# Sharing the group statistics of a normalisation between VectorE and ScalarE: 8 of 32 groups in five of eight chunks

## What is computed

```python
def _gn(v, G=32, eps=1e-5):
    g = v.reshape(B_, H_, W_, G, C_ // G)
    m = jnp.mean(g, axis=(1, 2, 4), keepdims=True)
    s = jnp.var(g, axis=(1, 2, 4), keepdims=True)
    return ((g - m) / jnp.sqrt(s + eps)).reshape(v.shape)

# layer 0: _L0_conv_ref is a layer norm over channels, five projections with sigmoid gates and masks,
#   einsum('bkjd,bkid->bijd', left, right), a layer norm, a projection and an output gate
x = x + _L0_conv_ref(_gn(x), ...)
# layer 1: 12 x 12 Fourier modes, mixed over channels
x = x + _L1_conv_ref(_gn(x), ...)
```

## Time and profile before

| | |
|---|---|
| median of 3 runs | 2864.22 us (2863.98 to 2865.37) |
| the profiled execution | 2871.38 us, its span 2869.6 us |
| granted TensorE clock, mean of the span | 0.959 of full speed |
| VectorE's statistics, first to last instruction | 14.71 to 193.97 us |
| last instruction of `prepare` | 202.12 us + 0.20 |
| DMA bytes moved per second while chunks are loaded | about 410 GB/s |

### The profile page before, as it was taken

How to read it: one execution, slowest core, us unless ns; L and a number is a source line. 1 busy time by engine, 2 the same in 40 slices (tenths; PEclk the granted TensorE clock), 3 DMA queues, 4 the chain that set the end, 5 groups by cost and what they waited for, 6 DMA issues and landing times. The chain is left out here.

```text
span 2869.6 us, 43971 instructions
## 1 busy us (share of the span) xinstructions
PE 2453.6 (86%) x14742; PEld 1996.0 (70%) x14742; DVE 2211.2 (77%) x3468; ACT 1380.6 (48%) x1812; POOL 1022.4 (36%) x1043
## 2 busy tenths in 40 slices
PE   0008999889989979999999998699999989979983
PEld 0007988778878868888888887366665656778872
DVE  6998999779779838888888888777676767427852
ACT  0107999779779966766667676122122222100000
POOL 0019888787788830000000000244444444300000
PEclk9999999999999989999999999799999999859997
DMA  9945999898888877777777777999999999539999
GB/s 384 389 170 189 352 348 351 304 336 303 310 328 310 318 294 264 282 288 274 285 273 283 287 275 277 349 391 416 391 415 392 416 383 393 143 127 388 420 421 411
DMA packets 244984, 927.61 MB, mean 323 GB/s; under 512 B 18009, under 2 KB 21593, under 8 KB 244442
## 3 DMA queue, kind: packets, MB, share of 16 engines
q1 hardware_dynamic: 205912, 796.12, 73.6%
q10 hardware_dynamic: 38898, 129.21, 11.3%
HBM read 527.85 MB, written 394.92 MB: 322 GB/s over the span
## 5 line engine op out<-in xcount | busy, mean ns | idle before, releaser
L1236 POOL TENSOR_TENSOR fi_square_sum<-fi_square_sum,fi_square 128x1024 f32<-128x1024 f32 x128 | 302.9, 2366 | 362.4 <-ACT fi_square L1202 362.4
L717 DVE SCALAR_TENSOR_TENSOR pj_lr<-pj_v_ps,keep_b_val,pj_sig 128x1024 f32<-128x1024 f32 x256 | 328.6, 1284 | 129.0 <-PE pj_v_ps L570 98.4
L1202 ACT ACTIVATE fi_square<-fi_x 128x1024 f32<-128x1024 f32 x128 | 135.4, 1058 | 519.8 <-DVE fi_x L1264 517.3
L510 POOL TENSOR_TENSOR front_ring<-front_ring,front_gn_shift 128x512 f32<-128x512 f32 x256 | 329.9, 1290 | 33.2 <-DVE front_ring L683 33.2
L653 ACT ACTIVATE pj_sig<-pj_g_ps,keep_b_gate 128x1024 f32<-128x1024 f32 x256 | 285.9, 1117 | 43.1 <-PE pj_g_ps L570 38.2
L1157 PE MATMUL fi_y_ps<-fi_scaled,keep_w_bd 128*128 128x512 f32 x512 | 273.4, 616 | 31.6 <-DVE fi_scaled L1247 31.1
L909 PE MATMUL ct_acc_ps<-ct_l_hi,ct_r_hi 128*128 128x512 f32 x1024 | 281.0, 395 | 17.4 <-ACT ct_r_hi L932 17.4
L913 PE MATMUL ct_acc_ps<-ct_l_lo,ct_r_hi 128*128 128x512 f32 x1024 | 280.8, 395 | 0.0
L917 PE MATMUL ct_acc_ps<-ct_l_hi,ct_r_lo 128*128 128x512 f32 x1024 | 280.1, 394 | 0.0
L1247 DVE TENSOR_TENSOR fi_scaled<-fi_m,fi_s_ps 128x512 f32<-128x512 f32 x256 | 174.2, 681 | 136.5 <-DMA fi_m<-mixed_d 127.6
L530 POOL TENSOR_TENSOR front_ring<-front_ring,pj_guess 128x512 f32<-128x512 f32 x256 | 267.4, 1046 | 3.3 <-POOL pj_guess L524 1.6
(11 more groups left out here) (183 smaller groups left out, 6313.2 us busy)
## 6 DMA issues: line engine op xcount, KB each, us to landing
lr_d<-pj_lr SPq DMA_DIRECT2D x128, 1024.0 KB, 6.4
gate_d<-pj_gout SPq DMA_DIRECT2D x128, 512.0 KB, 7.1
ct_l<-lr_d SPq DMA_DIRECT2D x64, 1024.0 KB, 7.0
ct_r<-lr_d SPq DMA_DIRECT2D x64, 1024.0 KB, 9.0
mixed_d<-ct_o SPq DMA_DIRECT2D x64, 1024.0 KB, 5.0
fi_g<-gate_d SPq DMA_DIRECT2D x128, 512.0 KB, 14.9
fi_x<-in_x SPq DMA_DIRECT2D x32, 2048.0 KB, 17.2
fi_m<-mixed_d SPq DMA_DIRECT2D x128, 512.0 KB, 17.6
```

Of the source, the lines that this page charges most:

```text
L510: pool.tensor_tensor(tile(m), tile(m), keep.gn_shift[:, :].unsqueeze(1).to_broadcast([P, WS // 2, C]), ALU.add).then_inc(shifted, 1)
L717: dve.scalar_tensor_tensor(out=out[:, :, RG * (m % 2):RG * (m % 2) + RG], in0=v_ps[:, :].rearrange("p (q i) -> p q i", i=RG), scalar=keep. ...
L1236: pool.tensor_tensor(square_sum[:, :, :], square_sum[:, :, :], square[:, :, :], ALU.add).then_inc(sum_done, 1)
```

## The change

VectorE leaves the last 8 of the 32 groups (`SG` = 8, `WG` = 24) of chunks 2 to 6 (`SHARED`) to ScalarE. For each such chunk and group, ScalarE runs two activations over the same 512 elements: Identity and Square, both with the bias `minus_pivot` (one value per partition and group) and with an accumulated sum (`accum_out`); the element-wise results go to two PSUM banks, `spill`, and are not read. Each activation waits for the one two before it. The pivot is the mean that `bn_stats` found for the first half of chunk 0; two VectorE instructions write it after chunk 0. ScalarE takes chunk 2 before its wait for `products`, and chunks 3 to 6 after its weight copies. The load of chunk i + 2 now also waits for ScalarE's part of chunk i (`spilled`).

Before the second half of chunk 7, VectorE turns the sums into means and sums of squared deviations and writes them into the slots of `stats` that `bn_stats` would have filled (`merge_shared`, 10 instructions). Chunk 6 is now taken in halves too, so `stats` has 12 slots: 8 of halves, 4 of wholes.

```diff
-HALVED = (0, 1, NCHUNK - 1)
+HALVED = (0, 1, NCHUNK - 2, NCHUNK - 1)
+SHARED = list(range(2, NCHUNK - 1))
+SG = 8
+WG = G - SG
...
+        spill = [t.ps(f"spill{b}", [P, STATS_T * CG]) for b in range(2)]
...
                 if i >= 2:
                     sp.wait_ge(chunk_done, i - 1)
+                    if i - 2 in SHARED:
+                        sp.wait_ge(spilled, 2 * SG * (SHARED.index(i - 2) + 1))
...
+            def shared(i):
+                b = i % 2
+                k = SHARED.index(i)
+                for h in range(2):
+                    act.wait_ge(x_loaded[b][h], DMA * (i // 2) + DMA)
+                for q in range(SG):
+                    part = xc[b][:, :, CG * (WG + q):CG * (WG + q) + CG]
+                    across = [bank[:, :].rearrange("p (t c) -> p t c", c=CG) for bank in spill]
+                    done = 2 * (SG * k + q)
+                    if done:
+                        act.wait_ge(spilled, done - 1)
+                    act.activation(across[0], part, ACT.Identity, bias=minus_pivot[:, q:q + 1],
+                                   accum_out=act_sum[:, q, k:k + 1]).then_inc(spilled, 1)
+                    if done:
+                        act.wait_ge(spilled, done)
+                    act.activation(across[1], part, ACT.Square, bias=minus_pivot[:, q:q + 1],
+                                   accum_out=act_square[:, q, k:k + 1]).then_inc(spilled, 1)
...
+            act.wait_ge(pivot_ready, 1)
+            shared(SHARED[0])
             act.wait_ge(products, 1)
...
+            for i in SHARED[1:]:
+                shared(i)
             act.wait_ge(root_in, 1)
...
+            def merge_shared():
+                n = CG * STATS_T
+                dve.wait_ge(spilled, 2 * SG * len(SHARED))
+                link(dve.tensor_scalar(act_mean[:, :, :], act_sum[:, :, :], 1.0 / n, None, ALU.mult))
+                link(dve.tensor_tensor(act_sum[:, :, :], act_sum[:, :, :], act_mean[:, :, :], ALU.mult))
+                link(dve.tensor_tensor(act_inner[:, :, :], act_square[:, :, :], act_sum[:, :, :], ALU.subtract))
+                link(dve.tensor_tensor(act_mean[:, :, :], act_mean[:, :, :],
+                                       pivot[:, :].unsqueeze(2).to_broadcast([P, SG, len(SHARED)]), ALU.add))
...
+                for e in (0, 3):
+                    at = slice(first + 1 + e, first + 6 * wholes, 6)
+                    dve.tensor_copy(stats[:, WG:G, at], act_mean[:, :, 0:wholes])
+                    at = slice(first + 2 + e, first + 6 * wholes, 6)
+                    dve.tensor_scalar(stats[:, WG:G, at], act_inner[:, :, 0:wholes], 0.5, None, ALU.mult)
+                for field, table, share in ((1, act_mean, 1.0), (2, act_inner, 0.25)):
...
+                    last = dve.tensor_scalar(stats[:, WG:G, at], whole, share, None, ALU.mult)
+                link(last)
...
             def statistics(i):
+                groups = WG if i in SHARED else G
                 if i in HALVED:
                     for h in range(2):
+                        if i == NCHUNK - 1 and h == 1:
+                            merge_shared()
...
-                        for g in range(G):
+                        for g in range(groups):
...
-            for i in range(3):
+            statistics(0)
+            dve.wait_ge(chunk_done, 1)
+            link(dve.tensor_copy(pivot[:, :], stats[:, WG:G, 1]))
+            dve.tensor_scalar(minus_pivot[:, :], pivot[:, :], -1.0, None, ALU.mult).then_inc(pivot_ready, 1)
+            for i in range(1, 3):
                 statistics(i)
```

More of the change, by code:

```diff
@@ L142, in prepare @@
         inner_sum = t.sb("inner_sum", [P, G])
+        pivot = t.sb("pivot", [P, SG])
+        minus_pivot = t.sb("minus_pivot", [P, SG])
+        act_sum = t.sb("act_sum", [P, SG, len(SHARED)])
+        act_square = t.sb("act_square", [P, SG, len(SHARED)])
+        act_mean = t.sb("act_mean", [P, SG, len(SHARED)])
+        act_inner = t.sb("act_inner", [P, SG, len(SHARED)])
         total = t.sb("total", [P, G])
@@ L150, in prepare @@
         chunk_done = t.sem("chunk_done")
+        pivot_ready = t.sem("pivot_ready")
+        spilled = t.sem("spilled")
         mean_ready = t.sem("mean_ready")
@@ L313, in _ @@
             link = chained(dve, step)
+            def merge_shared():
[6 more added lines that the diff above has]
+                                       pivot[:, :].unsqueeze(2).to_broadcast([P, SG, len(SHARED)]), ALU.add))
+                first = 6 * SPLIT
+                wholes = len(SHARED) - 1
+                halves = 6 * 2 * HALVED.index(SHARED[-1])
+                for e in (0, 3):
[4 more added lines that the diff above has]
+                for field, table, share in ((1, act_mean, 1.0), (2, act_inner, 0.25)):
+                    at = slice(halves + field, halves + 12, 3)
+                    whole = table[:, :, wholes:wholes + 1].to_broadcast([P, SG, 4])
+                    last = dve.tensor_scalar(stats[:, WG:G, at], whole, share, None, ALU.mult)
+                link(last)
             def statistics(i):
                 b, done = i % 2, DMA * (i // 2) + DMA
+                groups = WG if i in SHARED else G
                 if i in HALVED:
                     for h in range(2):
+                        if i == NCHUNK - 1 and h == 1:
+                            merge_shared()
                         dve.wait_ge(x_loaded[b][h], done)
```

## The result

| | before | changed |
|---|---|---|
| median | 2864.80 us (10 runs) | 2857.22 us (10 runs, 2855.45 to 2859.23) |
| ratio | | 0.9974, 95% interval 0.9965 to 0.9984 |
| the profiled execution | 2871.38 us | 2859.01 us |
| first normalisation of `project` in it | 202.89 us | 193.50 us |

The change is faster by 7.6 us, which is 0.26%; by the interval it is between 4.6 and 10.0 us. The prediction was 10.2, and its range (2851.0 to 2858.0) holds the median.

What follows compares the result with a forecast made beforehand. Loads were taken to bound `prepare` until chunk 6, then VectorE. Statistics ending 10.5 us earlier, less 0.4 in the tail, gave 10.2 us off 2864.22: 2854.0 us, range 2851.0 to 2858.0 (80 in 100).

Steps and rivals of the forecast that it cites:

- a part taken back by the merge or behind `prepare`: Rival: a dearer merge or later stages take back part, leaving a gain of 4 to 8 us; 8 in 100.
- VectorE's path from chunk 6 on is the bound: End of `prepare`: VectorE alone sets the pace to `gn_scale`; whatever is cut there moves all that follows as a block.
- VectorE's share: VectorE's statistics on shared chunks: 24 groups take 14.3 us instead of 19.07 whole, 7.9 instead of 10.5 per half.
- The pivot: After chunk 0 on VectorE: two small instructions and a wait, some 0.5 us, covered by idle time, costing the path nothing.
- ScalarE's share: Sixteen activations per shared chunk on ScalarE at 0.61 to 0.96 us each; 0.81 taken, 13.0 us a chunk.
- The rival with slow strided reads: ScalarE reads 8-byte pieces at half rate, 20 us a chunk, so no change at 2864.9 us; 7 in 100.
- No table load among them: ScalarE's Identity and Square activations on shared chunks need no table load between them; none was counted.
- The rule for the loads: Chunk loads in `prepare`: a chunk arrives at the later of 20.4 us after its predecessor and 23.5 after issue.
- The late-issue half: Chunk loads in `prepare`: a chunk issued late is there 23.5 us after its issue, which waits for the freed buffer.
- The merge and the tail: VectorE before and after chunk 7's last half: ten merge instructions cost 1.6 us, larger tail passes 0.4 us.
- Nothing behind `prepare` absorbs the shift: Stages after `prepare`: everything shifts as a block, so the 10.1 to 10.2 us gain reaches the end.
- The slower rival: ScalarE becomes the bound above 20 us a chunk: 26 us slower, or some 60 with table loads; together 5 in 100.

Runs made afterwards that it cites:

- three kernels that were built to depend on it: Changed kernel with ScalarE taking 12 groups, 14 groups, or 8 with every activation issued twice; first normalisation at 195.04, 202.96 and 210.46 us.
- the same kernel with 3 more instructions: Changed kernel plus 3 unused statistics instructions in the tail; 8.4 us faster than the kernel before, ratio interval 0.9960 to 0.9983.
- 14 groups: Changed kernel with ScalarE taking 14 groups of each shared chunk instead of 8; median 0.2 us below the kernel before, ratio interval 0.9992 to 1.0009.
- 8 groups, doubled: Changed kernel with every ScalarE activation of the shared chunks issued twice; median 6.5 us above the kernel before, ratio interval 1.0014 to 1.0032.
- the two kernels that were timed twice: The changed kernel, 7.6 and 6.1 us faster than before, and it with ScalarE also sharing chunk 7, 9.4 and 10.7 us faster.

## Why the prediction was right, and where it was off

- **The number.** It is right in part by luck. The median lies near the high end of the range, and the causes that the prediction gave for that end did not occur: ScalarE's price was 11.3 us a chunk and not 18, the merge 1.55 us and not 3.8. The two samples of the gain, 7.6 and 6.1 us, both lie outside the gain of 8.5 to 12 us that was given 80 in 100. They fall where the prediction put 8 in 100, a part taken back by the merge or behind `prepare`. The first block alone, with 9.4 us, does what was forecast.
- **VectorE's path from chunk 6 on is the bound, and what it loses moves the whole program.** Right: no idle time from 131.06 to the end of the statistics; first normalisation 9.4 us earlier where 10.1 to 10.2 were forecast.
- **VectorE's share.** 14.33 us a chunk (14.3), 15.75 for chunk 6 in halves (two times 7.9).
- **The pivot.** It took 0.4 us, and the idle time ahead of chunk 1 shrank to 0.34 us: free, as forecast.
- **ScalarE's share.** 11.3 us a chunk instead of 13.0. The read-out of the sum is an instruction of its own, as assumed, but with its overlap it adds only 0.09 us to the 0.61 of the activation, where 0.20 was taken. On the path this is worth nothing. The rival with slow strided reads fell: 0.61 us up to the read-out is the price of the earlier trace rows for contiguous data. The rule of the Trainium skill's page "SBUF — State Buffer" (section "Door 1: The DMA port swizzle (why `[64,N]` ≈ `[32,N]`)") that speaks of a penalty for each crossing to a new 16-byte line does not show in the time of these activations; but each line gets the two accesses here that the same passage asks for, so this does not refute it.
- **No table load among them.** Right. Between 27.27 and 162.89 ScalarE has none.
- **The rule for the loads.** The late-issue half held within 0.5 us in three kernels that were built to depend on it. The other half is the step that failed, "A chunk that is queued in time follows the one before it in 20.4 us": chunk 5 took 21.4, because the prediction has no term for a load of instructions that holds up one DMA engine by 1 us. It cost 1.1 us at chunk 5 (131.06 for 130.0), and, as VectorE's small terms came out short by 0.2, 0.9 us at the end of the statistics (184.28 for 183.4).
- **The merge and the tail.** 1.55 us (1.6) and 0.3 us (0.4). The merge fills slots of `stats` of six numbers a group, three for each of the two interleaved streams.
- **Nothing behind `prepare` absorbs the shift.** Not contradicted, but not shown to the last tenth either: kernels from -11.5 to +7.6 us follow the shift to within 3 us, with a slope of 0.91. The missing 1.8 us of the median (7.6 of 9.4) is the larger part of the error of 2.6 us. Its cause is not settled: it appeared again in a second sample of the same kernel and was absent from the same kernel with 3 more instructions.
- **The slower rival.** The deciding price of 20 us a chunk was right: level at 19.7 (14 groups), 6.5 us slower at 22.5 (8 groups, doubled).

## What to carry to other kernels

When loads are paced by the engine that frees the buffers, moving work to an idle engine pays twice, in fewer late issues and in a shorter backlog at the end, up to the price at which the helper frees the buffers last; write both times down as recurrences before choosing the share. A split into halves is worth only what the engine waits for the second half: 0.4 us in the first block while it was behind, 3.6 us once it was ahead. A pace read from a few rows holds as long as nothing else uses the DMA engines: look for the loads of instructions among the queues too. And when a change of some us in a kernel of 2860 us is to be judged, read the length of the block in the profile, which repeated to 0.3 us, beside a median whose gain repeated to 1.3 and 1.5 us in the two kernels that were timed twice.

## What the runs showed of the hardware

- Loads of instructions use the DMA engines that move the data. One packet of 8 KB took 0.34 us, and the two data packets of 4 KB behind it 0.50 and 0.49 instead of 0.16, so that one engine lost about 1 us (changed kernel, 113.35 to 114.65 us). A chunk spread over 16 engines is there only with its slowest one: it came 21.4 instead of 20.4 us behind the one before. If the engine that is held up has time to spare, nothing shows (135.07). DMAs queued without a gap did not slow the engines otherwise: their last landing came every 10.2 us for each half chunk of 4 MiB.
- An accumulated sum on ScalarE costs an instruction of 0.19 us, of which 0.09 us is seen (0.70 us from one activation of 512 elements to the next, 0.49 for 256). Pieces of 8 bytes at a step of 256 bytes cost ScalarE nothing over contiguous data (0.61 us up to the read-out, 0.61 in the earlier trace rows), and VectorE's `bn_stats` on the same tile at the same time kept its 0.60 us (14.33 for 24, before the change 19.07 for 32).
